# A Trainium2 decoder block: how GpSimd's row scatters and VectorE's routing are spread over the expert tiles

## The reference

```
x = layernorm(x + attention(x))                      # 16 heads of 16
x = layernorm(x + cross_attention(x, ctx))           # one head, softmax over 77
gate = softmax(x @ gate_w + gate_b)                  # 8 experts
topv, topi = top_k(gate, 2);  topv = topv / topv.sum(-1)
out = sum over e of  weight_e * (relu(x @ w1[e] + b1[e]) @ w2[e] + b2[e])
x = layernorm(x + out)
```

## Time and profile before

| | |
|---|---|
| median of 3 runs | 1446.65 us (1446.23 to 1447.54) |
| the profiled execution | 1446.49 us |
| its span, first to last instruction | 1444.3 us |
| TensorE (PE) busy | 1402.0 us, 97% |
| VectorE (DVE) busy | 1077.0 us, 75% |
| ScalarE (ACT) busy | 863.8 us, 60% |
| GpSimd (POOL) busy | 554.9 us, 38% |
| mean granted TensorE clock | 0.995 |

### The profile page before, as it was taken

How to read it: one execution, slowest core, us unless ns; L and a number is a source line. 1 busy time by engine, 2 the same in 40 slices (tenths; PEclk the granted TensorE clock), 3 DMA queues, 4 the chain that set the end, 5 groups by cost and what they waited for, 6 DMA issues and landing times.

```text
span 1444.3 us, 48788 instructions
## 1 busy us (share of the span) xinstructions
PE 1402.0 (97%) x18538; PEld 931.5 (65%) x18538; DVE 1077.0 (75%) x1963; ACT 863.8 (60%) x1973; POOL 554.9 (38%) x952
## 2 busy tenths in 40 slices
PE   8999999999999999999999999999999999999995
PEld 4355455544445445444444448888899999999994
DVE  5888888888888888888999965767556555555553
ACT  3588888877777877878878784333333333333331
POOL 1211222222222225321125212577775555555554
PEclk9999999999999999999999999999999999999998
DMA  4335455533434223322333232222322222222221
GB/s 159 97 100 184 146 162 166 141 118 107 123 118 131 84 74 114 104 72 68 110 106 108 71 121 109 70 84 89 126 97 81 73 74 74 76 73 71 78 74 51
DMA packets 108031, 147.44 MB, mean 102 GB/s; under 512 B 27258, under 2 KB 79786, under 8 KB 106778
## 3 DMA queue, kind: packets, MB, share of 16 engines
q1 hardware_dynamic: 93658, 105.71, 24.3%
q0 software_dynamic: 14000, 38.11, 7.8%
q10 hardware_dynamic: 144, 0.52, 0.1%
HBM read 81.09 MB, written 63.17 MB: 100 GB/s over the span
## 4 chain that ended last, share of the span: by engine, by line
PE 81%; DVE 8%; issue 5%; POOL 3%; ACT 1%; DMA 1%; DVEq 0%; SPq 0%; POOLq 0%; ACTq 0%
PE pa L905 15%; PE pa L1141 14%; PE pb L905 13%; PE po L1081 13%; PE pb L1155 13%; PE px L905 6%; DVE neg L1427 3%; PE px L898 2%; PE po L898 1%; PE pb L898 1%; ACT w_sb L1258 1%; PE po L1012 1%; PE px L987 1%; PE px L961 1%; POOL y_parts L852 1%
## 5 line engine op out<-in xcount | busy, mean ns | idle before, releaser
L1427 DVE TENSOR_REDUCE neg<-pa 128x1 f32<-128x1024 f32 x512 | 611.4, 1213 | 81.2 <-PE pa L905 73.1
L1258 ACT ACTIVATE w_sb<-pb 128x512 f32<-128x512 f32 x996 | 590.1, 599 | 104.4 <-PE pb L905 69.2
L905 PE MATMUL pb<-w_sb 99*32 99x512 bf16 x3984 | 391.9, 380 | 4.2 <-ACT w_sb L1258 2.1
L1371 ACT ACTIVATE space<-pa,b1T_sb 128x128 f32<-128x128 f32 x568 | 154.7, 383 | 322.6 <-PE pa L1141 320.0
L905 PE MATMUL pa<-w_sb 96*32 96x512 bf16 (+1 forms) x4208 | 322.9, 380 | 6.0 <-DVE neg L1427 6.0
L1081 PE MATMUL po<-w_sb,space 128*32 128x256 f32 x4000 | 304.5, 379 | 0.0
L1141 PE MATMUL pa<-xgT,attn_t 128*128 128x128 f32 x2272 | 269.0, 275 | 0.8 <-DVE attn_t L1737 0.8
L1141 PEld LDWEIGHTS pa<-xgT,attn_t 128*128 128x128 f32 x2272 | 266.0, 192 | 5.9 <-issue 2.5
L1155 PE MATMUL pb<-w_sb,space 128*128 x1136 | 261.7, 381 | 0.0
L1155 PEld LDWEIGHTS pb<-w_sb,space 128*128 128x128 f32 x1136 | 209.9, 191 | 25.5 <-issue 0.3
L1081 PEld LDWEIGHTS po<-w_sb,space 128*32 128x32 f32 x4000 | 124.1, 111 | 98.8
(11 more groups left out here) (243 smaller groups left out, 1227.7 us busy)
## 6 DMA issues: line engine op xcount, KB each, us to landing
y_parts<-attn_t SPq DMA_DIRECT2D x13, 896.0 KB, 5.5
w_sb<-w SPq DMA_DIRECT2D x17, 512.0 KB, 5.9
attention_out<-space SPq DMA_DIRECT2D x64, 128.0 KB, 2.2
w_sb<-w SPq DMA_DIRECT2D x7, 1024.0 KB, 8.1
xg<-x_by_expert SPq DMA_DIRECT2D x54, 130.0 KB, 2.1
q_parts<-w_sb SPq DMA_DIRECT2D x48, 128.0 KB
w_sb<-q_parts SPq DMA_DIRECT2D x64, 96.0 KB, 3.6
w_sb<-k_parts SPq DMA_DIRECT2D x64, 96.0 KB, 3.5
```

The lines of the kernel that those rows point to most:

```text
L905: mm = pe.matmul(out[at:end], lhsT[:, at:end], rhs, start=start, stop=stop, tile_position=(0, at))
L1258: act.activation(ex_of(n)[:, half * HALF:(half + 1) * HALF], score_bank(n, half), ACT.Exp, scale=SCALE).then_inc(e_done, 1)
L1371: ins = act.activation(hT[tile % 2][:, f, :], pH[tile % 2][:, f, :], ACT.Relu, bias=g.b1_sb[:, bass.ds(e * FT + f, 1)])
L1427: dve.tensor_reduce(neg[i % 2][:, t:t + 1], pa[n % 2][:, :], AX.X, ALU.max, negate=True).then_inc(max_done, 1)
```

## The change

The row scatters of a batch go through a new helper, `send_rows(since, n)`, called at two places of each tile: with n = 0 where they stood, ahead of `spread_3`, and with n = 1 behind `scatter_out`, at the end of the tile. Each call issues one scatter instead of two. Batch B - 2 is sent in tiles 5 to 12, batch B - 1 in tiles 13 to 20, each one tile later than before; `reweight` stands ahead of the ninth, in tiles 9 and 17. For batch B - 2, `positions` moves in tile 3 behind the logits and `best`, and `rows` and `weights` move to tile 4. The scatter of the last tile's y, which nothing reads, is left out. The wait for all output rows moves from GpSimd to SyncE.

```diff
@@ SyncE, end
+                sp.wait_ge(out_rows, 16 * FFN_TILES)
@@ GpSimd
+                def send_rows(since, n):
+                    for b, at in ((B - 2, 3), (B - 1, 3 + TB)):
+                        t = 2 * (since - at) + n
+                        if 0 <= t < TB:
+                            scatter_first(b, t)
+                        t -= TB
+                        if t == 0:
+                            reweight(b)
+                        if 0 <= t < TB:
+                            scatter_second(b, t)
...
-                    if 2 <= since < 6:
-                        scatter_first(B - 2, 2 * (since - 2))
-                        scatter_first(B - 2, 2 * (since - 2) + 1)
-                    if 6 <= since < 10:
-                        if since == 6:
-                            reweight(B - 2)
-                        scatter_second(B - 2, 2 * (since - 6))
-                        scatter_second(B - 2, 2 * (since - 6) + 1)
...
+                    send_rows(since, 0)
                     if tile:
                         spread_3(tile - 1)
...
                     gather(tile)
                     if tile:
                         scatter_out(tile - 1)
-                scatter(FFN_TILES - 1)
+                    send_rows(since, 1)
+
                 spread_3(FFN_TILES - 1)
                 scatter_out(FFN_TILES - 1)
-                pool.wait_ge(out_rows, 16 * FFN_TILES)
@@ VectorE
-                    if tile == SHIFT + 1:
-                        positions(B - 2)
-                        rows(B - 2)
                     if MAIN_GATE <= j - 1 < NT:
...
                     if tile == SHIFT:
                         hot_experts(B - 2)
                     if tile == SHIFT + 1:
+                        positions(B - 2)
+                    if tile == SHIFT + 2:
+                        rows(B - 2)
                         weights(B - 2)
```

## The result

| | before | after |
|---|---|---|
| median, both kernels run in turn (22 runs each) | 1446.84 us | 1448.92 us (1447.0 to 1450.79) |
| ratio after to before | | 1.0015, 95% interval 1.0008 to 1.0021 |
| the profiled execution | 1446.49 us | 1448.87 us |
| its span | 1444.3 us | 1446.8 us |
| mean granted TensorE clock | 0.995 | 0.995 |

What follows compares the result with a forecast made beforehand. TensorE, busy nearly the whole span, was taken as the bound, leaving only its waits and the tail. Routing -0.4, scatters +3.45 and tail -1.5 gave +1.55 on the median 1446.65: 1448.2 us, range 1444.0 to 1450.7.

Steps and rivals of the forecast that it cites:

- Routing: Tiles 4 and 5: spreading batch B-2's routing over three tiles only divides the work; gain 0.4 us, bounds 0 and 0.8.
- the lower bound's pause: Routing's bound of 0 gain: the register load before `result` takes longer behind an idle engine.
- Scatters in tiles 6 to 10: Second scatter place delays `spread_2`: tile 6 loses 0.76, tiles 7 to 9 2.01, tile 9 regains 1.20, tile 10 loses 1.44.
- a sum of 11.30: Expert-tile loop from `spread_3` to `spread_3`: 10.02 us, with a row scatter inside 11.30, 0.67 over the 10.63 period.
- The batch that ends a tile later: Batch B-1's second half ends in tile 20: loss 0.44 us, from TensorE's wait for the w1 copy; bounds 0 and 1.68.
- set at nothing: Behind tile 11, the new order of y's scatter, row scatter and gather within a tile was priced at no cost.
- The tail: Kernel end: with the wait on SyncE, GpSimd's DRAIN runs beside the landing; gain 1.5 us, bounds 0 and 1.67.
- rival 1: Kernel end: GpSimd's DRAIN counts from the landing, so the tail does not shorten; +3.05, 1449.7 us; chance 0.18.
- Rival 2: Expert tiles: the scatter's move is hidden and `spread_2` is not delayed; -3.1, 1443.5 us; chance 0.12.
- Rival 3: Tile 10: the late transpose becomes a TensorE gap of about 1.9 us, lowering the clock; +3.2, 1449.9 us; chance 0.08.
- Rival 4: Load at 1026.5 comes earlier and half its stall and clock loss goes; sum -0.35, 1446.3 us; chance 0.12.

Runs made afterwards that it cites:

- the two kernels of the table: The changed kernel unaltered, 1448.63 us, and one with both row scatters first and batch B-2's routing as before, 1446.02 us; the kernel before took 1446.21 us.
- the pads spread: Changed kernel with both row scatters first and SyncE's eight pad stores one to a tile in tiles 13 to 20: 1444.77 us against 1446.21 for the kernel before.

## Why the prediction was right, and where it was wrong

The total was right: +2.1 us measured against +1.55. The mechanisms were those named, and their sizes were off. The loss from the batch that ends later was 1.4 to 2 us too small in the sum, and the gain of routing was 0.2 too large. Against these stand the gain of the tail, which was 0.75 too small, and the loss in tiles 6 to 10, which was 0.8 too large. That these nearly cancel is luck; no part of the working says that they should.

**Routing, forecast -0.4: measured -0.20, and -0.17 between the two kernels of the table that differ by it in these tiles.** As the step said, the work is only divided. Tile 5's wait for `mix` is 1.08, forecast 1.3. The missing 0.2 is the lower bound's pause: VectorE stood 0.26 us (released by issue) ahead of `result` in tile 4, where in the kernel before it went on without a gap, and `norm_3` to the projection took 2.70 us (917.34 to 920.04) instead of 2.48.

**Scatters in tiles 6 to 10, forecast 3.01: measured 2.18.** Tile 6 cost 0.97 (0.76), tiles 7 and 8 0.48 and 0.47 (0.67 each), tile 9 -0.68 (0.67 - 1.20 = -0.53), tile 10 0.94 (1.44). The loop was read right, 11.11 us against a sum of 11.30. The link that was too long is the `spread_1` pair: the sum took 0.08 + 1.22 from a tile in which it started behind a pause; started at once it takes 956.97 to 958.06, 1.08. From the end of that pair to `spread_3` it was 2.79 (958.06 to 960.85) instead of 0.03 + 2.84, and from `spread_3` to y's scatter, less the row scatter, 4.09 instead of 3.99. The row scatter's 1.28 was exact (953.53 to 954.81).

**The batch that ends a tile later, forecast 0.44: measured 1.8 to 2.4 on chips A.** This is the step that failed. The two bounds were 0 and 1.68, and the text took the row nearest by kind, a wait of 0.44, instead of asking whether GpSimd had any time left from tile 15 on. It has almost none: in the kernel before, from 1027 to 1070 us, the one pause on GpSimd longer than 0.4 us is the 0.89 inside `reweight`. In the changed kernel (GpSimd's timeline, first a gather, then the first second choice behind `reweight`; below it VectorE's):

```profile
1045.69 1.09 POOL L831 DMA_INDIRECT space<-y_parts,y_tags  x1 [2.10 <-DMA y_parts<-space,y_tags]
...
1052.65 1.00 POOL L781 DMA_INDIRECT x_by_expert<-pay,pos_i  x1 [0.89 <-POOL pay L776]
1053.67 0.20 POOL L837 TENSOR_TENSOR c_all<-c_all,neg_half 128x1 f32<-128x1 f32 x1
1053.95 0.57 POOL L839 TENSOR_TENSOR c_all<-c_all,neg_half 128x1 f32<-128x1 f32 x1
```

```profile
1054.56 0.41 DVE L1824 TENSOR_SCALAR space<-space,c_all 128x256 f32<-128x256 f32 x1 [4.30 <-POOL c_all L839]
...
1056.73 1.31 DVE L1735 COPY attn_t<-w_sb 128x1024 f32 x2
```

`spread_3` starts as the row scatter ends; VectorE had waited 4.30 us for it, its copy of w1 is behind that, and TensorE's 1.30 us at 1057.57 is the wait for the copy. The gather of 1045.69 shows something that the prediction had set at nothing: with one row scatter behind it instead of two, y's scatter has not landed when the gather wants it, and GpSimd idles 2.10 us (1.53 at another gather, at 1028.57). That looks like the cause, but it isn't: with both scatters first there is no such wait, and tiles 18 to 22 lose 2.42 all the same. On a full queue the whole 2.56 us of two more scatters counts, less what slack VectorE and TensorE have; the 1.8 to 2.4 measured lie under that. Even the upper bound, which took off 0.88 us of idle time, was too low. The price holds where GpSimd's queue is what TensorE waits for: on a chip B, where other waits come first, no loss showed.

**The tail, forecast -1.5 with bounds 0 and 1.67: measured -2.25 in two profiles of the changed kernel, -1.7 with the wait moved alone.** The place was right and rival 1 is refuted: the DRAIN runs beside the landing. The move of the wait gave the upper bound; the other 0.6 is a shorter DRAIN. The forecast kept its length, and the length changes with the program. It also starts 0.2 us ahead of the last scatter's execution, not within 0.3 us of its end.

**The rivals.** Rival 1 (the tail gives nothing): no, the wait alone gives 1.7 in the traces. Rival 2 (the move is hidden): no, every transpose of x2 in tiles 6 to 10 waits, and less only when the scatter is taken away. Rival 3 (the gap in tile 10 lowers the clock): not in this kernel, whose gap is 1.48 us; but with both scatters first the gap is 2.0, and there the clock can fall (below). Rival 4 (the load stall halves): no, 2.28 us.

## What to carry to other kernels

Where an engine is a link in a loop between others, count the loop from one round to the next; an operation that nobody waits for must stand where the loop leaves that engine idle, and moved ahead of the loop's next link it costs its length less the slack, each round. Where an engine has no idle time over a stretch, added or delayed work is priced at its full length, and the price is paid at the end of the stretch; how much of it the bounding engine sees depends on its other waits (here 1.8 to 2.4 us on chips A and none on a chip B). At the end of a kernel, put the wait for the last transfers on an engine whose DRAIN is short (SyncE's took 7 ns behind it), and let the long DRAIN run beside them.

## What the runs showed of the hardware

A stop of TensorE near 2 us may or may not be followed by a low clock, and its length alone does not decide. The kernel with both scatters at the second place had four such stops in the same place of four tiles, of 2.91, 2.32, 2.00 and 1.98 us (the timeline above). The windows view of the 4 us behind each:

```profile
core 0: us, PE busy (x) PEld busy (x) DVE busy (x) ACT busy (x) POOL busy (x), PEclk, DMA share, GB/s
976.20:980.20 4.00, 4.00 (x27) 3.67 (x28) 2.90 (x8) 0.74 (x2) 1.14 (x3) 1.00 0.10 25
988.95:992.95 4.00, 4.00 (x27) 3.69 (x28) 2.90 (x8) 0.74 (x2) 1.14 (x3) 1.00 0.14 33
1001.36:1005.36 4.00, 4.00 (x14) 3.23 (x15) 2.84 (x7) 0.75 (x2) 1.14 (x3) 0.60 0.14 33
1015.44:1019.44 4.00, 4.00 (x13) 3.24 (x14) 2.84 (x7) 0.74 (x2) 1.14 (x3) 0.57 0.10 33
```

The two longer stops left the granted clock at 1.00; behind the two shorter ones it was 0.60 and 0.57, mostly the lower level of 1.2 GHz, and TensorE did 13 or 14 matmuls in the time of 27. Tile 10 tells the same of two kernels: behind a stop of 2.00 us with the pads spread, and of 2.01 us with both first and the old routing, the windows are

```profile
987.50:992.00 4.50, 4.43 (x17) 3.81 (x17) 2.80 (x7) 0.37 (x1) 2.86 (x5) 0.64 0.30 91
```

```profile
987.50:992.00 4.50, 3.12 (x19) 2.86 (x20) 3.27 (x8) 0.80 (x3) 3.01 (x6) 1.00 0.28 88
```

(the second holds the last 1.38 us of the stop), and tile 10 took 12.21 us in the one and 10.68 in the other. The load's stall was followed by 0.56 to 0.60 after 2.10, 2.27 and 2.28 us, and by full speed after 2.01 us in the kernel with both first and the old routing, whose tile 15 took 9.51 us instead of 11.23 to 11.45. So each such stop carries 1.5 to 1.7 us that may be paid or not. Over all profiles, in the expert tiles up to 1250 us: behind the stops of 0.95 to 1.76 us the clock was full over the next 4 us; behind the 15 from 1.98 to 2.91 us it was full five times and 0.57 to 0.65 ten times; behind the nine of 3.97 us or more it was 0.50 to 0.60. The chance of 0.08 that the forecast gave to this in tile 10 was for a gap of 1.9; the 1.48 that came left the clock full.

GpSimd's DRAIN is the other surprise: 2.5 to 10.5 us in all, within each group of like programs the same to 2 ns at the end of the block (6015 and 5770 ns on both kinds of chip), and not tied to transfers alone.
